# Attention steps of a one-core transformer block: the projection of a coming batch moved behind the maxima, its read-out moved one step on

## What is computed

```python
xn = _layernorm(x)
projected = einsum('bte,fe->btf', xn, in_proj_weight)     # q, k, v
attention = einsum('bhtd,bhkd->bhtk', q / sqrt(8), k) + causal mask
x1 = einsum('bhtk,bhkd->bhtd', softmax(attention), v)
attn = einsum('bte,fe->btf', x1, out_proj_weight)
ffn  = shared_expert(xn) + sum over the top 2 of 7 experts of w_e * expert_e(xn)
out  = x + attn + ffn
```

## Time and profile before

| what | before |
|---|---|
| median of three runs | 512.21 us |
| the profiled execution | 512.13 us |
| its span in the profile | 510.1 us |
| TensorE busy | 458.3 us (90%) |
| VectorE, ScalarE, GpSimd busy | 350.2, 306.4, 296.1 us |
| mean granted TensorE clock | 0.935 of full speed |
| attention steps, first to last exponential | 44.9 to 294.3 us |

### The profile page before, as it was taken

How to read it: one execution, slowest core, us unless ns; L and a number is a source line. 1 busy time by engine, 2 the same in 40 slices (tenths; PEclk the granted TensorE clock), 3 DMA queues, 4 the chain that set the end, 5 groups by cost and what they waited for, 6 DMA issues and landing times.

```text
span 510.1 us, 12198 instructions
## 1 busy us (share of the span) xinstructions
PE 458.3 (90%) x3919; PEld 328.0 (64%) x3923; DVE 350.2 (69%) x722; ACT 306.4 (60%) x661; POOL 296.1 (58%) x424
## 2 busy tenths in 40 slices
PE   8888998989878887878898999989899999979996
PEld 4766555646555554555565667868668788858874
DVE  6796998868766565665555048757667687656897
ACT  2756776757665565665555667646547676546653
POOL 1445997968767567667677540255364497856300
PEclk9999999979998699898756699999999999989999
DMA  9786999897753454355237024767767668730762
GB/s 249 234 256 216 317 317 308 289 377 252 249 158 110 124 147 153 96 159 152 89 106 273 22 86 141 228 207 226 242 210 247 223 195 279 246 119 28 227 196 72
DMA packets 60412, 99.80 MB, mean 196 GB/s; under 512 B 11045, under 2 KB 29226, under 8 KB 59328
## 3 DMA queue, kind: packets, MB, share of 16 engines
q1 hardware_dynamic: 55872, 90.57, 56.0%
q0 software_dynamic: 4480, 8.47, 4.9%
HBM read 60.85 MB, written 38.94 MB: 196 GB/s over the span
## 4 chain that ended last, share of the span: by engine, by line
PE 65%; ACT 8%; issue 5%; SPq 5%; another core or an unknown queue 5%; DVE 4%; DMA 2%; ACTq 0%; DVEq 0%; POOL 0%
PE ps L894 11%; PE ps L892 11%; PE ps L893 10%; PE ps L1042 6%; PE ps L975 6%; PE ps L983 5%; ACT sb_work L767 3%; PE ps L1046 3%; PE ps L1025 2%; PE ps L1210 2%; SPq L494 2%; PE ps L971 2%; PE ps L1027 2%; DMA sb_ring<-qk 2%
## 5 line engine op out<-in xcount | busy, mean ns | idle before, releaser
L1416 DVE TENSOR_REDUCE sb_blockmax<-ps 128x6 f32<-128x768 f32 x128 | 121.3, 955 | 67.2 <-PE ps L983 61.9
L767 ACT ACTIVATE sb_work<-ps 128x768 f32<-128x768 f32 x128 | 104.0, 813 | 79.2 <-PE ps L971 60.8
L663 POOL DMA_INDIRECT ys<-sb_v_all,sb_xn_all x76 | 79.3, 1043 | 76.0 <-DVE sb_v_all L1543 57.1
L635 POOL TENSOR_SCALAR_AFFINE_SELECT sb_work<-sb_work 128x512 f32<-128x512 f32 x128 | 82.2, 643 | 56.1 <-ACT sb_work L767 54.7
L893 PE MATMUL ps<-sb_ring,sb_wb 128*128 128x512 f32 (+5 forms) x231 | 83.2, 360 | 0.0
L975 PE MATMUL ps<-sb_ring 32*128 32x256 f32 x256 | 53.0, 406 | 29.4 <-ACT sb_work L767 23.2
L1521 DVE TENSOR_TENSOR sb_v_all<-ps,sb_v_all 128x512 f32<-128x512 f32 (+3 forms) x93 | 57.2, 615 | 25.7 <-ACT sb_v_all L839 10.4
L613 POOL DMA_INDIRECT xs<-sb_xn_all,sb_posu x64 | 62.2, 972 | 13.7 <-issue 13.7
L975 PEld LDWEIGHTS ps<-sb_ring 32*128 32x128 f32 x256 | 26.5, 196 | 60.3 <-issue 52.1
L983 PE MATMUL ps<-sb_mask_b,sb_ident_b 128*128 128x256 bf16 x256 | 55.1, 301 | 0.0
L839 ACT ACTIVATE sb_v_all<-ps 128x512 f32<-128x512 f32 (+3 forms) x93 | 49.5, 532 | 9.0 <-PE ps L894 5.4
(11 more groups left out here) (165 smaller groups left out, 1063.0 us busy)
## 6 DMA issues: line engine op xcount, KB each, us to landing
sb_wb<-wd SPq DMA_DIRECT2D x50, 384.0 KB
sb_ring<-qk SPq DMA_DIRECT2D x64, 256.0 KB
wd<-sb_wb SPq DMA_DIRECT2D x8, 1088.0 KB, 5.2
sb_wb<-wd SPq DMA_DIRECT2D x25, 320.0 KB
xs<-sb_o_all SPq DMA_DIRECT2D x19, 260.0 KB, 3.6
qk<-sb_ring SPq DMA_DIRECT2D x32, 128.0 KB
sb_work<-ys SPq DMA_DIRECT2D x16, 256.0 KB, 3.2
sb_xn_all<-xs SPq DMA_DIRECT2D x15, 260.0 KB
```

Source lines behind the costliest of these rows:

```text
L635: pool.affine_select(out=o, in_=o, compare_op=ALU.is_ge, fill=0.0, base=0, pattern=[[0, 4], [1, 128]], channel_multiplier=-1)\
L663: pool.indirect_dma_start(out=ys_d, out_offset=bass.IndirectOffsetOnAxis(ap=row, axis=0), in_=yst[i % NYS][:, EMB * j:EMB * j + EMB], in_o ...
L767: act.activation(part.rearrange("p (k h q) -> p h k q", h=2, q=128), ps[:, 4:6, 0:HEAD].rearrange("p h (k q) -> p h k q", q=128), ACT.Exp, ...
L1416: dve.tensor_reduce(blockmax[:, p % 2, q, a:b + 1, 0:3], ps[:, a:b + 1, 0:HEAD].rearrange("p h (k c) -> p h k c", c=128), AX.X, ALU.max).t ...
```

## The change

In even steps at or above 0 both blocks of the value sums now stand in the first gap, and the projection stands at the end of the step, behind the maxima. The projection's high part is copied out on ScalarE in the following odd step, between its two exponentials and ahead of the copy of values. The low part is taken on VectorE in that odd step, behind its first maximum. The steps below 0, and those above 48 without a projection, keep their order.

```diff
@@ ScalarE, between the two exponentials (k = 1) @@
-                        if k and projected(n) is not None:
-                            projection_high(n)
+                        if k and n and projected(n - 1) is not None:
+                            projection_high(n - 1)
@@ TensorE, step(n) @@
-                if projected(n) is not None:
+                if n < 0 and projected(n) is not None:
                     project(n)
                 if isq(n - 1):
                     value_sums(n - 1, 0)
-                    if projected(n) is None:
-                        value_sums(n - 1, 1)
+                    value_sums(n - 1, 1)
                 if isq(n) or isq(n + AHEAD):
                     scores(n, 1)
-                if isq(n - 1) and projected(n) is not None:
-                    value_sums(n - 1, 1)
                 if 0 < n < NQ + 2 and n % 2:
                     across(n)
                 if n >= 0 and isq(n + 2):
                     maxima(n + 2)
+                if n >= 0 and projected(n) is not None:
+                    project(n)
@@ VectorE, step(n), behind maximum(0) @@
-                if n >= 0 and projected(n) is not None:
-                    projection_low(n)
+                if n > 0 and projected(n - 1) is not None:
+                    projection_low(n - 1)
```

## The result

In 13 executions each, the changed kernel took 515.23 us (median) and the kernel before 512.79. The ratio is 1.0092, with a 95% interval from 1.0049 to 1.0135: **slower**, by just under 1%, or 2.5 to 6.9 us of some 512. The ratios in this document compare only executions in the faster of the two states that a kernel runs in, so they are not the quotients of the medians. The profiled execution took 513.14 us with a span of 511.1 us and a mean granted clock of 0.933. Forecast were 511.0 us, which is 1.2 us less than before, and no difference beyond 1%.

The account below looks back on a forecast made before the run. TensorE's program was taken as the bound, except SyncE's queue from 72.4 to 99.1 us. Terms -2.5 + 1.0 + 0.3 = -1.2 us took 512.13 to 510.9, median 511.0 us; range 505.5 to 516.5.

Parts of the forecast that it names:

- the value sums: TensorE, even steps: second block directly behind the first saves 0.14 us in each of 18 steps, 2.5 us together.
- the late stores: SyncE's queue: stores wait for low keys, delaying loads; 1.0 us for step 13, 0.3 for steps 1, 5 and 21.
- the odd wait: Rival: ScalarE's 1.79 us wait for scores in some twelve odd steps ends, saving 16 us, to 496; chance 0.05.
- Bound and chain: Whole kernel: SyncE's queue bounds from 72.4 to 99.1 us; elsewhere the chain follows TensorE's program.
- the maxima's earlier end: Even step's second gap: maxima come 0.36 us sooner, and ScalarE's copies with them, adding up to 0.12 us saved.
- The read-out in odd steps: Odd steps: TensorE's wait for the low part is covered by 0.12 us, so cost 0, upper end 2.4 us.
- SyncE's stores: SyncE's queue: stores start 1.60 us behind the first exponential; later loads cost 1.0 us plus 0.3 us.
- this case: The author's own forecast for the whole kernel: 511.0 us, 508 to 514 with single terms at their ends; chance 0.50.
- the stores that hold SyncE's queue: Rival, steps with j = 1: loads behind late stores land after TensorE needs them, 514 to 518.2 us; chance 0.20.
- ScalarE's pace: Rival: ScalarE bounds even steps at 2.90 us instead of 3.46, saving 10 us, to 502; chance 0.07.
- The clock: Rival: three half-clock steps more or fewer are 6 us, 517 or 505; chance 0.08 more, 0.10 fewer.

Follow-up runs that it names:

- e2: The changed kernel with the new order only in even steps 0 to 18, against the kernel before: 467.58 us, ratio 1.0078.
- e3: The changed kernel with SyncE's five stores, from step 0 on, behind the loads of their step, against the kernel before: 465.49 us, ratio 1.0039.
- c1: The kernel before with the value sums' second block directly behind the first, projection still ahead of both: 465.66 us, ratio 1.0032 to the kernel before.
- i1: The changed kernel, stores behind loads, GpSimd masking only one of four diagonal blocks (not usable), against the kernel before: 449.42 us, ratio 0.9694.
- g1: The changed kernel, stores behind loads, each even step's second mask on VectorE from step 24, against the kernel before: 495.87 us, ratio 0.9679.
- h3: The kernel before with GpSimd masking only the first of four diagonal blocks (not usable): 454.06 us, ratio 0.9774 to the kernel before.
- h2: The changed kernel with the light mask, GpSimd masking only one of four diagonal blocks (not usable), against the kernel before: 497.75 us, ratio 0.9829.

## Why the prediction was wrong, point by point

The forecast was -2.5 us for the value sums, +1.0 and +0.3 for the late stores. Two of these terms failed. The stores of step 1, priced together with those of steps 5 and 21 at 0.3 us, cost about 3 us on their own: 28.38 us from step 0 to 8 in e2 against 25.44 in e3, on one chip. And the saving of 2.5 us did not arrive: from step 24 to 60 it was 0.0 us on the chip of the result and a loss of 1.3 on chips A and B, single executions all. On chip A the value sums had to wait for GpSimd's masks, and on the other two the odd wait took the saving back. The forecast had neither wait.

**Bound and chain.** Half right. The chain does follow TensorE's program outside 72 to 99 us. But I read from it that a shorter order on TensorE is worth its length. With GpSimd 83.88 us busy of 123 I never asked which loop runs through its sends and masks where the step gets short.

**Value sums, 0.14 us a step.** TensorE's part was right: the chain of the changed kernel shows 0.57 + 0.22 = 0.79 us for the two blocks, against 0.93. The second block took 0.22 us directly behind the first, as in odd steps. The Trainium skill (TensorE: Matmul & The Clock Gate, The mechanism) has weight loads overlap only with matmuls on other row groups; both blocks use all rows, and by that rule the saving would be 0. The trace differs, and it decides. The second block's weight loads start while the first block's matmuls are running (their ends are modelled):

```profile
140.77 0.64 PE L1042 MATMUL ps<-sb_work 128*32 128x256 f32 x8
141.01 0.35 PEld L1046 LDWEIGHTS ps<-sb_work 128*32 128x32 f32 x8
```

The same section also lets a load run ahead into the background weight buffer; whether that is what happens here no run tells. The step's saving was mis-sized: where nothing waits it is 0.5 us, not 0.14. The missing part is in the second gap, where I had said that the maxima's earlier end is worth 0.12 at most. ScalarE's copies waited for them 0.44 us and took the gap to 1.80.

**What the moved block delays.** This is a step of the sum that had no term at all. I took the second block as work that costs its own time wherever it stands. Ahead of the scores it also delays the second exponential, its mask, and through GpSimd the sums of the next even step, which had nothing to spare: in the old order they start 145.39 - 145.27 = 0.12 us behind the masks' end, and 0.10 us where they wait for it in e3. On the chips without the odd wait this takes back the whole saving from step 24 on. Shown by e3's and e2's rows, by c1 (8.0 us of waiting in 18 steps), and from the other side by i1 and g1.

**The read-out in odd steps, 0.** Right on the chip of the result for plain steps, where the odd wait covers it. TensorE waits 0.4 us each in three places for the low part from 44 to 132 us, 1.2 in all; the end I gave was 2.4. Where there is no odd wait the 0.12 us of cover were not there: odd steps of i1 take 3.08 to 3.10 us and 2.95 in turn, those of h3 2.95 and 2.91. Over 24 odd steps that makes 12 x 0.15 + 12 x 0.04 = 2.3 us, an estimate, so the term belonged at its upper end.

**SyncE's stores.** This term failed. Their start was right: in step 13 the first store stands at 94.37 us, 1.66 behind the first exponential at 92.71, where I had 1.60. The price of steps 1, 5 and 21 was 0.3 us together, because "the quads are loaded several steps ahead of use". I took that for seven. The first use is three steps on, and three steps are 9.3 us (from 55.09 to 64.39 before), while the load in question took 8.29 us to land. With the stores later it was issued 1.7 us later and landed more slowly; TensorE idled 1.75 us for it and then ran at half clock. The load that ends SyncE's part of the chain was issued at 102.77 and landed after 8.02 us, 3.7 later than the earlier trace rows, where I expected 1. The upper end of 6.9 held it, but the range of 508 to 514 that I gave for this case did not: with 6.9 in place of 0.3 the sum is 517.5. That e3 and i1 lose nothing by step 8 shows that the order in SyncE's queue is the cause. Why the loads land more slowly behind it was not shown.

**Rivals.** The one that came true is the first, the stores that hold SyncE's queue, to which I gave 0.20 and 514 to 518 us; 515.23 lies in it. ScalarE's pace did come, 2.95 us in even steps, and gave nothing. The odd wait did not go: 1.84 us for 1.79, as I had argued against it. The clock is not ruled out as a part of the loss. The two profiled executions have 0.933 and 0.935, but on chip B the executions compared have 0.928 to 0.947 after the change and 0.943 to 0.966 before. Waits and half clock come together here (67 to 70 us above), and no run separates them.

**What stays open.** What the odd wait is. It follows steps in which GpSimd issues two sends, and the trace calls it "remote" or names a matmul that was long done. On the chip of the result and on chip B it ends mostly 4.5 to 4.9 us behind the even step's second exponential in either order. With the light mask (h2) it is 4.2 to 4.3, shorter by about what the mask is shorter. Measured from the end of GpSimd's second send it is 0.6 to 0.7 us in every odd step of h2 from 25 to 59, and 0.6 to 1.4 in the kernel before. Two rows of h2:

```profile
139.98 0.96 POOL L613 DMA_INDIRECT xs<-sb_xn_all,sb_posu  x1 [0.30 <-issue]
141.59 0.81 ACT L767 ACTIVATE sb_work<-ps 128x768 f32<-128x768 f32 x1 [1.48 <-PE ps L971]
```

So it follows GpSimd's sends, by a path that the trace does not show. It takes the even steps' saving back on those chips before GpSimd's loop can. Spreading the sends was only run on chips that don't have it. How much of g1's gain comes from a shorter odd wait rather than from the loop was not separated.

## What to carry to other kernels

A piece of work that moves ahead of another delays all that hangs on the other: follow that chain through the helper engines until it comes back to the engine it left, add up the loop, and compare it with the period that the change aims at (here 6.54 us round GpSimd against 5.9 of work). Read for each gap which engine ends it: here ScalarE's copies, not TensorE. And where stores stand in a queue ahead of loads, price their lateness by how far ahead of their first use the loads behind them are issued, against the time they take to land in the trace. Here seven steps ahead were three, and 9.3 us against 8.3.

## What the runs showed of the hardware

The same kernel, the one before, took 464 us on three chips and 506 to 513 us on two others and on the chip of the result. Its mean granted clock was 0.98 to 1.00 on the first three, 0.93 to 0.97 on the two others and 0.935 in the profiled execution on the last. Odd waits like those of 1.79 and 1.84 us in plain pairs of steps are on the slower ones only. An indirect send holds GpSimd for 0.97 us with 0.16 before it, or 0.30 before a second one in a row. GpSimd's mask of 128x512 takes 0.64 us, of 128x128 0.29. The three loads of a quad that end SyncE's part of a chain above took 7.93, 8.02 and 8.29 us to land, with the DMA engines 99% busy or more meanwhile. After TensorE had idled 1.75 us for one of them, its granted clock was 0.57 from 67 to 70 us, and 1.00 before the change. Weight loads of a block of matmuls started 0.24 us behind the start of the block before it, on the same rows.
